# Projections of the second layer as three fp32r products of halves, with jobs moved in the written-out order

## The reference

```python
h = film(rmsnorm(x, norm1_w), cond, film1_w, film1_b)
Q = h @ q_w + q_b
K = h @ k_w + k_b
V = h @ v_w + v_b
scores = jnp.einsum('bnd,bmd->bnm', Q, K) * D ** (-0.5)
attn = jax.nn.softmax(scores, axis=-1)
out = jnp.einsum('bnm,bmd->bnd', attn, V)
x = x_in + (out @ proj_w + proj_b)
```

## Time and profile before

| | us |
|---|---|
| median of 3 runs | 879.87 |
| the profiled execution | 880.76 |
| its span, first to last instruction | 878.9 |
| TensorE busy | 838.7 (95%) |
| VectorE busy | 666.1 (76%) |
| ScalarE busy | 459.4 (52%) |
| POOL busy | 227.3 (26%) |

### The profile page before, as it was taken

One profiled execution on the slowest core, in us unless ns is written; L12 is line 12 of the kernel. 1 busy time (PEld: TensorE's weight loads), 2 busy tenths in 40 slices (PEclk: granted clock), 3 DMA queues, 4 the chain that ended last, 5 costly groups with the idle time before them and its releaser, 6 DMA issues.

```text
span 878.9 us, 13287 instructions
## 1 busy us (share of the span) xinstructions
PE 838.7 (95%) x4978; PEld 521.8 (59%) x4978; DVE 666.1 (76%) x1139; ACT 459.4 (52%) x840; POOL 227.3 (26%) x377
## 2 busy tenths in 40 slices
PE   6999999999999999999989989999999999999994
PEld 3668888958977998887845433333333333333342
DVE  8998657676538577646458879999999999999377
ACT  4646232144332443333232158888878878888760
POOL 4443412202002103112112710233333333333411
PEclk9999999999999999999989969999999999999998
DMA  8613122110000000000597600505050505000002
GB/s 314 252 49 97 55 92 98 49 52 2 1 1 1 1 1 1 2 1 1 168 182 193 252 1 3 92 21 92 21 93 21 92 21 93 23 27 24 27 25 73
DMA packets 29379, 57.40 MB, mean 65 GB/s; under 512 B 7228, under 2 KB 15152, under 8 KB 29314
## 3 DMA queue, kind: packets, MB, share of 16 engines
q1 hardware_dynamic: 22596, 44.40, 19.2%
q0 software_dynamic: 6720, 12.15, 4.7%
HBM read 39.26 MB, written 14.91 MB: 62 GB/s over the span
## 4 chain that ended last, share of the span: by engine, by line
PE 83%; DVE 8%; ACT 5%; POOL 2%; issue 2%; DMA 0%; DVEq 0%; ACTq 0%; POOLq 0%
PE PA L1531 15%; PE PA L1542 15%; PE PD L1327 10%; PE PA L1305 8%; PE PA L1253 7%; PE PD L1502 7%; PE PA L1408 5%; PE PD L1378 4%; PE PA L1246 2%; PE PA L1398 1%; PE PD L1600 1%; DVE NMX L2045 1%; PE PA L1477 1%; ACT R L1107 1%; PE PD L1253 1%
## 5 line engine op out<-in xcount | busy, mean ns | idle before, releaser
L2045 DVE TENSOR_REDUCE NMX<-PD 128x2 f32<-128x1024 f32 x256 | 301.9, 1220 | 25.7 <-PE PD L1502 21.2
L1107 ACT ACTIVATE R<-PA 128x512 f32<-128x512 f32 x512 | 267.0, 603 | 71.6 <-PE PA L1531 69.8
L1531 PE MATMUL PA<-STKR 50*128 50x512 f32 x512 | 185.3, 454 | 3.6 <-ACT R L1107 2.5
L1531 PEld LDWEIGHTS PA<-STKR 50*128 50x128 f32 x512 | 83.2, 188 | 151.7 <-ACT R L1107 139.3
L1502 PE MATMUL PD<-STKR 48*128 48x512 f32 x512 | 150.0, 456 | 4.2 <-DVE NMX L2045 4.1
L1043 ACT ACTIVATE R<-PA,VEC 128x512 f32<-128x512 f32 x64 | 43.8, 687 | 104.1 <-PE PA L1305 91.6
L1327 PE MATMUL PD<-WHR,HSR 128*128 128x256 f32 x512 | 95.3, 285 | 0.5 <-DVE HSR L1918 0.5
L1327 PEld LDWEIGHTS PD<-WHR,HSR 128*128 128x128 f32 x512 | 82.1, 191 | 6.1 <-issue 2.0
L1305 PE MATMUL PA<-XSR,WHR 128*128 128x512 f32 x256 | 81.2, 398 | 3.9 <-issue 2.0
L1502 PEld LDWEIGHTS PD<-STKR 48*128 48x128 f32 x512 | 62.0, 188 | 30.1 <-DVE NMX L2045 13.4
L1327 PE MATMUL PD<-WLR,HSR 128*128 128x256 f32 x256 | 72.4, 283 | 0.0
(11 more groups left out here) (288 smaller groups left out, 1181.3 us busy)
## 6 DMA issues: line engine op xcount, KB each, us to landing
STKR<-qk_terms SPq DMA_DIRECT2D x32, 384.0 KB, 8.8
R<-in_l_w SPq DMA_DIRECT2D x8, 1024.0 KB, 5.0
W<-in_w SPq DMA_DIRECT2D x4, 1024.0 KB, 10.7
qk_terms<-PARTS SPq DMA_DIRECT2D x8, 512.0 KB, 3.4
qk_terms<-PARTS POOLq DMA_DIRECT2D x8, 512.0 KB, 3.8
S<-row_reciprocals POOLq DMA_DIRECT2D x56, 64.0 KB, 2.1
X<-in_x SPq DMA_DIRECT2D x4, 512.0 KB, 8.5
qk_terms<-PARTS SPq DMA_DIRECT2D x8, 256.0 KB, 5.0
```

Source lines behind the costliest of these rows:

```text
L1107: act.activation(PB[:, n % 2, j, :], PA[:, e % NEB, :], ACT.Exp).then_inc(s_exp3, 1)
L1531: pe.matmul(PA[:, e % NEB, :], KS[rows, slot(gg), jj, kt * P:(kt + 1) * P], QS[rows, slot(gg), jj, c * HALF:(c + 1) * HALF], start=True, s ...
L2045: ve.tensor_reduce(out, PD[:, o:o + NROW, :], axis=AX_X, op=ALU.max, negate=True).then_inc(s_mred, 1)
```

## The change

Q, K and V products of layer 1 become three fp32r products of halves. The halves of the tiles go to XSR (the MLPs' tile halves, free at that time), those of the weights to the upper parts of C2 and S2 and back over WA. VectorE gets two new stages, tile_halves and weight_halves, and a subtraction in wv. The stage n1 of batch 0 moves to behind down product 29, wh stands behind 27. The adapter jobs ad and lr are moved later, and three max jobs stand between the Q/K jobs 8 to 15 in place of the end.

```diff
--- before.py
+++ after.py
@@ -103,14 +103,14 @@
 
 assert NLCH == 8 and TWO == P // GCOL
 SCHED = [("nr", 0), ("nn", 0), ("gk", 0), ("ba", 0), ("n0", 0), ("sx", 1), ("bu", 0), ("gg", 0), ("sq", 1), ("cg", 0), ("as", 0), ("bu", 1), ("gr", 0), ("gg", 1),
-         ("an", 0), ("nn", 1), ("ya", 0), ("n0", 1), ("ad", 0), ("gc", 0), ("cg", 1), ("y0", 0), ("yn", 0), ("ad", 1), ("bu", 2),
-         ("ad", 2), ("ws", 0), ("bu", 3), ("yn", 1), ("gk", 1), ("lr", 0), ("bg", 0), ("ma", 0), ("ya", 1), ("lr", 1),
-         ("y0", 1), ("mb", 0)]
-FIRST = mlps(0, "m", {0: [None, ("ws", 1), ("yn", 2), ("yn", 3), None, ("lr", 2)], 4: [("lr", 3)], 6: [("gb", 0)],
+         ("an", 0), ("nn", 1), ("ya", 0), ("n0", 1), ("gc", 0), ("cg", 1), ("y0", 0), ("ad", 0), ("yn", 0), ("bu", 2), ("ad", 1),
+         ("ws", 0), ("bu", 3), ("yn", 1), ("gk", 1), ("bg", 0), ("ma", 0), ("ya", 1), ("ad", 2), ("y0", 1), ("lr", 0), ("mb", 0)]
+FIRST = mlps(0, "m", {0: [None, ("ws", 1), ("yn", 2), ("yn", 3), None, ("lr", 1)], 2: [("lr", 2)], 5: [("lr", 3)], 6: [("gb", 0)],
                       8: [None, None, None, ("lr", 4)], 11: [("lr", 5)], 13: [("lr", 6)], 16: [None, None, None, ("lr", 7)]},
-             {NTILE - 1: [("h0", 0)], B * NTILE - 6: [("wt", 0)], B * NTILE - 4: [("wv", 0)]})
+             {NTILE - 1: [("h0", 0)], B * NTILE - 6: [("wt", 0)], B * NTILE - 5: [("wh", 0)], B * NTILE - 4: [("wv", 0)],
+              B * NTILE - 3: [("n1", 0)]})
 SCHED += FIRST[1:] + [("h0", 1)]
-SCHED += [("n1", 0), ("qk", 0), ("lb", 0), ("att", 0), ("az", 0), ("n1", 1), ("ao", 0), ("qk", 1), ("pr", 0), ("pn", 0),
+SCHED += [("qk", 0), ("lb", 0), ("att", 0), ("az", 0), ("n1", 1), ("ao", 0), ("qk", 1), ("pr", 0), ("pn", 0),
           ("att", 1), ("ws", 2), ("az", 1)]
 SECOND = mlps(1, "n2", {0: [None, ("pr", 1), ("pn", 1)]},
               {NTILE: [("x2", 0)], NTILE + 1: [("a1", 0)], NTILE + 2: [("g", 0)], NTILE + 3: [("a2", 0)], NTILE + 4: [("f2", 0)],
@@ -131,12 +131,16 @@
 
 TURN = {turn_step(m): m for m in range(1, NUNIT)}
 SOLO = turn_step(NUNIT - 1) + 1
-SCHED += weave([("qk3", QJOBS + j) for j in range(QJOBS - 1)], [("mx", EARLY + j) for j in range(QJOBS - 1)])
-EARLY += QJOBS - 1
-assert UNIT == EARLY
-SCHED += [("qk3", 2 * QJOBS - 1), ("mx", EARLY), ("tm", 0)]
-SCHED += weave([("v3", TWO + j) for j in range(TWO)], [("mx", EARLY + 1 + j) for j in range(TWO)])
-SCHED += [("mx", n) for n in range(EARLY + 1 + TWO, LEAD)]
+for j in range(QJOBS):
+    SCHED += [("qk3", QJOBS + j), ("mx", EARLY)]
+    EARLY += 1
+    if j % 2 and j < QJOBS - 1:
+        SCHED.append(("mx", EARLY))
+        EARLY += 1
+    if UNIT < EARLY <= UNIT + 2 and ("tm", 0) not in SCHED:
+        SCHED.append(("tm", 0))
+SCHED += weave([("v3", TWO + j) for j in range(TWO)], [("mx", EARLY + j) for j in range(TWO)])
+SCHED += [("mx", n) for n in range(EARLY + TWO, LEAD)]
 AFTER = {SOLO + 2 * j + i: [(("p3a", "p3")[i], j)] for j in range(TWO - 1) for i in range(2)}
 AFTER[SOLO + TWO - 1] += [("st", 0), ("end", 0), ("ea", 0)]
 AFTER[SOLO + TWO] += [("eb", 0)]
@@ -300,6 +304,9 @@
             R0, XN0, WA0, C20 = 8192, 33024, 37120, 41216
             STKR = at("STKR", R0, [P, NPLACE * 4096])
             PARTS = [at(f"PARTS{u}", o, [P, 2, 2, HALF]) for u, o in enumerate((XN0, WA0))]
+            WAR = at("WAR", WA0, [P, 4, KB, D])
+            C2R = at("C2R", C20, [P, T])
+            S2R = at("S2R", C20 + T, [P, T])
             NMT = at("NMT", C20, [UNIT, NPART, P])
             ONES = at("ONES", C20 + NPART * P, [P, 32])
             VR = at("VR", R0, [P, 2, NT * D])
@@ -401,6 +408,9 @@
                   for n, low in enumerate((QLR, KLR)))
         V = [VR[:, x, :].rearrange("p (t d) -> p t d", t=NT) for x in range(2)]
         PX = R[:, 4096:6144].rearrange("p (s n) -> p s n", s=2)
+        XTR = XSR[:, :].rearrange("p (b k t) -> p b k t", b=B, k=KB)
+        WQKV = [[a.rearrange("p (k n) -> p k n", k=KB), WAR[:, w]]
+                for w, a in enumerate((C2R[:, KB * D:T], S2R[:, KB * D:T], C2R[:, 0:KB * D]))]
         WVT = C2[:, 0:KB * D].rearrange("p (k n) -> p k n", k=KB)
         VBC = S2[:, 0:KB * P].rearrange("p (k m) -> p k m", k=KB)
         X2T = [flat(XN[:, 1]).rearrange("p (k t) -> p k t", k=KB), XT[:, 1]]
@@ -497,6 +507,8 @@
         s_z = sem("states_ready")
         s_zc = sem("states_cos_ready")
         s_zs = sem("states_sin_ready")
+        s_half1 = sem("second_layer_tile_halves_ready")
+        s_whalf = sem("attention_weight_halves_ready")
         s_rowbias = sem("v_bias_in_rows")
         s_qkh = sem("scores_operands_high_ready")
         s_vhi = sem("v_high_ready")
@@ -1361,11 +1373,18 @@
                 m.then_inc(s_afull, 1)
 
             def qk(b):
-                for name, w in (("q", 0), ("k", 1)):
+                pe.wait_ge(s_whalf, 2)
+                terms = [(k, w, x) for k in range(KB) for w, x in TERMS]
+                for name, weights in zip("qk", WQKV):
                     for c in range(NC):
-                        xt_ready(b, "n1", c)
+                        pe.wait_ge(s_half1, (b * NC + c + 1) * KB)
                         for k in range(KB):
-                            project(abank(b, name, c, k), WA[:, w], k * P, b, c, s_afull)
+                            o = abank(b, name, c, k)
+                            for n, (i, w, x) in enumerate(terms):
+                                m = pe.matmul(o, weights[w][:, i, k * P:(k + 1) * P],
+                                              XTR[:, (1 - b, b)[x], i, c * HALF:(c + 1) * HALF],
+                                              start=(n == 0), stop=(n == len(terms) - 1))
+                            m.then_inc(s_afull, 1)
 
             def scores(b, t):
                 if t == 0:
@@ -1383,11 +1402,12 @@
                 if b == 0 and j == 0:
                     evacuated(pe, 0, "wv", 0)
                 o = abank(b, "v1", j)
+                terms = [(k, w, x) for k in range(KB) for w, x in TERMS]
                 for u in range(2):
                     t = 2 * j + u
-                    for k in range(KB):
-                        m = pe.matmul(o[:, u * D:(u + 1) * D], XT[:, b, k, t * P:(t + 1) * P], WA[:, 2, k, :],
-                                      start=(k == 0), stop=(k == KB - 1))
+                    for n, (k, w, x) in enumerate(terms):
+                        m = pe.matmul(o[:, u * D:(u + 1) * D], XTR[:, (1 - b, b)[x], k, t * P:(t + 1) * P], WQKV[2][w][:, k, :],
+                                      start=(n == 0), stop=(n == len(terms) - 1))
                 m.then_inc(s_afull, 1)
 
             def probs_turn(b, t):
@@ -1949,12 +1969,30 @@
                 ve.tensor_copy(VBC.rearrange("p k m -> p (k m)"), bank_of(b, "wt", 1)[:, 0:KB * P]).then_inc(s_aevd, 1)
 
             def wv(b):
-                ve.tensor_copy(WA[:, 2].rearrange("p k d -> p (k d)"), bank_of(b, "wv", 0)).then_inc(s_aevd, 1)
+                high, low = (a.rearrange("p k n -> p (k n)") for a in WQKV[2])
+                o = bank_of(b, "wv", 0)
+                link(ve.tensor_copy(high, o))
+                ve.tensor_tensor(low, o, high.bitcast(F32), ALU.subtract).then_inc(s_aevd, 1)
                 row = BC[:, BP, :]
                 ve.wait_ge(s_bin, 16)
                 ve.tensor_tensor(row, bank_of(b, "wv", 1)[:, 0:D], row, ALU.add).then_inc(s_aevd, 1)
                 evacuated(ve, b, "wv", 1)
                 ve.sem_inc(s_rowbias, 1)
+
+            def weight_halves(_):
+                ve.wait_ge(s_wain, 32)
+                for w in range(2):
+                    high, low = WQKV[w]
+                    link(ve.tensor_copy(high, WA[:, w]))
+                    ve.tensor_tensor(low, WA[:, w], high.bitcast(F32), ALU.subtract).then_inc(s_whalf, 1)
+
+            def tile_halves(b):
+                for _, tag, h, k in turned(b, "n1"):
+                    evacuated(ve, b, tag, h, k)
+                    high, low = (XTR[:, x, k, h * HALF:(h + 1) * HALF] for x in (1 - b, b))
+                    tile = XT[:, b, k, h * HALF:(h + 1) * HALF]
+                    link(ve.tensor_copy(high, tile))
+                    ve.tensor_tensor(low, tile, high.bitcast(F32), ALU.subtract).then_inc(s_half1, 1)
 
             def scores_max(b, t):
                 ve.wait_ge(s_sfull, b * NT + t + 1)
@@ -2120,7 +2158,7 @@
             run({"ws": low_weights, "pn": lambda b: normalise("pr", b, False),
                   "cg": gated_maps, "as": ada_stats, "an": ada_normalise, "ad": hidden_rows, "gc": grouped_columns, "bu": bu,
                  "ya": y0("ya"), "y0": y0("y0"), "ma": split("ma"), "mb": split("mb"), "m": split("m"), "n2": split("n2"), "u0": split("u0"),
-                 "u1": split("u1"), "d0": d0, "h0": h0, "lb": lb, "wt": wt, "wv": wv, "qk": qk, "att": att("att"), "az": att("az"),
+                 "u1": split("u1"), "d0": d0, "h0": h0, "lb": lb, "wt": wt, "wh": weight_halves, "wv": wv, "n1": tile_halves, "qk": qk, "att": att("att"), "az": att("az"),
                  "ao": att("ao"), "pr": pr, "d1": d1,
```

## The result

The changed kernel takes 887.52 us (median of 7 runs, 882.18 to 888.03); the kernel before took 880.42 beside it (7 runs, 879.1 to 882.11). The ratio is 1.0063, 95% interval 1.0044 to 1.0083: 5.5 us slower, and above the forecast range. (The means are 5.6 us apart, the medians 7.1: four of the seven runs of the changed kernel lie at 887.5 to 888.0 and three at 882.2 to 885.3.) The profiled execution took 887.91 us, span 886.1, mean granted clock 0.977 (before 880.76, 878.9 and 0.982).

The account below looks back on a forecast made before the run. Products on TensorE were taken to bound the second layer's stretch (25.5 of 25.7 us busy). Against the profiled 880.76 us, +2.2 +0.9 +1.7 -2.7 -1.9 = +0.2, in the median's terms 880.1 us; range 875.5 to 883.8.

Parts of the forecast that it names:

- Three max jobs: Moved from the end to between Q/K jobs: -3.4 at the end, +1.3 and +0.2 among the jobs, sum -1.9 us.
- It just keeps up: Between the Q/K jobs: VectorE needs 4.8 us for two jobs against TensorE's 4.8; 0.2 put for small waits.
- the clock behind the end: Half clock level at the start of the loop of steps, 9.8 us in the profile, left as it is.
- Batch 0: Second layer: TensorE waits 4.9 us for a bank before K, +0.9 us; clock then at half level, +1.7.
- Batch 1 and behind it: Second layer: Q and K take 11.1 instead of 13.75 us, -2.7 kept; the V saving (0.9 to 1.2) lost.
- Adapter: First layer: +1.2 us ahead of mb's transposes, +1.0 for one more lr product in the MLP, sum +2.2.
- the rival that it does not come: Start of the steps: the half clock level behind the tail does not come; 876.7 us, chance 0.10 including ending soon.
- its other half (it ends soon): Same rival's other case: the half level at the start of the steps ends soon; 876.7 us, shared chance 0.10.
- The forecast's +0.2: Whole kernel: sum of all terms against the profiled 880.76 us; 880.1 us as a median, no measurable change, chance 0.46.
- The rival on the slower side: Batch 0, first Q job's bank: pairs of 1.5 us, wait 6.7 us, second half-clock stretch; 883.6 us, chance 0.22.

Follow-up runs that it names:

- max_only: The kernel before with only the change's three max jobs moved between the Q/K jobs; 883.41 us, ratio 1.0024.
- h0_behind_qk: The changed kernel with h0 of batch 1 moved behind batch 0's Q/K job; 879.81 us, ratio 0.9984.
- products_only: The changed kernel with the adapter jobs and the max jobs back in the order of the kernel before; 881.45 us, ratio 1.0013.
- adapter_early: The kernel before with the adapter jobs in the change's order, except ad 1 ahead of bu 2 again; 887.71 us, ratio 1.0079.
- turn_later: The changed kernel with the turn of the first 16 maxima moved one Q/K job later; 882.03 us, ratio 1.0014.
- adapter_lr_only: The kernel before with only ad 2 and the lr products moved, ad 0 and ad 1 in their old places; 881.45 us, ratio 1.0014.

## Why the prediction was wrong

**Three max jobs: the step that failed.** The prediction had -1.9; the jobs alone measure +2.1. Its reductions were counted rightly: with the turn out of the way they give 1.4 between C and D. "It just keeps up" was worked out for the products and reductions of a pair, as load. The turn of the maxima was not in the working at all. With the three jobs added it stands as the third in a row that takes one of two pairs of banks, and so it waits for the reduction of the first of them and what is queued ahead of that on VectorE: 1.94 us. That this place costs the time is shown: the intervals with the turn here and one Q/K job later don't meet. Behind a wait of that size the clock may fall too: in the kernel after the next four products took 3.65 us instead of 1.9. The 1.3 by which C-D grew is -1.4 for the fewer reductions, 0.9 for the turn's place (max_only and h0_behind_qk against the kernels with the later turn) and 1.8 for the fall. The trace of max_only explains -0.45 without a fall and about +1.3 with one. What remains up to its 2.1 is open. A candidate is a longer half level in the steps (the clock behind the end, below): with the 371.7 us from D to the end that the kernel after and h0_behind_qk have, it would be 2.8 more. No trace of max_only shows it.

**Batch 0: right mechanism, too small.** Predicted +2.6 with the clock; from A to B the kernel after lost 4.77, of which 1.25 is the lr product, so 3.5; products_only alone lost 3.97. Q began 4.6 us behind the transposes, as worked out. What was too small is the wait, 5.11 (4.9 predicted), and above all K, which took 7.8 us in the kernel after and 8.3 in products_only (7.2 by the terms). The cause is confirmed: h0 1 moved by one place, and the wait went to 1.73 and the fall away.

**Batch 1 and behind it: right.** -2.7 predicted; Q and K of batch 1 take 2.83 less, and from B to C kernels with the new products need 216.2 (median of eight), those without 219.6 (of six), so the 2.7 is kept and part of the V saving may be too. The new products cost 0.228 us each in the long row of 48, a little under the 0.231 taken. By the Trainium skill (FP8 and Floating Point Precision, TensorE Precision Notes) a true fp32 product takes four passes; three products of halves against four passes would be 0.75, as an estimate. Here the ratio is 10.92 / 13.75 = 0.79, so the measured rows decide.

**Adapter: right in size and mechanism, with one path missed.** +2.2 predicted, +2.3 alone. Split as predicted (1.2 ahead of mb, 1.0 in the MLP) it measures 1.07 and 1.25. The gelu waits behind bu 2's job on VectorE and W1's halves behind it, as worked out: 55.92 against 55.3, the low half at 58.17 against 57.75 (the terms written there add up to 57.71), VectorE's idle 2.34 against 2.4. What the prediction missed is ad 0's copy: it counted TensorE's 1.49 us wait for ad 0 as removed, and did not follow that copy to who reads it. Behind y0 0's statistics it comes 7 us later, TensorE stands 1.22 us for it, and it makes the plain repair (adapter_early) worse than the fault.

**The clock behind the end: there, but not for nothing.** The prediction left it as it is, a term of 0. The half level came in all 14 traces, so the rival that it does not come is out. Its length differs, though: TensorE worked 13.6 us at it behind D in the kernel after, 10.8 in the kernel before, and 3.4 in max_only and turn_later, so its other half (it ends soon) did happen in kernels with the same shorter end. In the profiled execution D-end is 2.7 of the 7.2 us lost. The shorter end took waiting away from that stretch and left the work in it, which fits; but whether the longer stretch comes from the change or by chance is not shown by one trace each.

**Sum.** In the timed ratios adapter +2.3, products +1.1 and max jobs +2.1 make 5.5, and the change measures 5.5; each of these is known to 1.1 to 1.7 us. The forecast's +0.2 is off mainly by the 4 us of the max jobs and the 1.2 of the products. The rival on the slower side had the right place (the bank of the first Q job) and the wrong price: pairs stayed at 1.06 us (177.49 to 181.75 for four). My list had no case in which two terms were late together.

## What to carry to other kernels

When a product gets cheaper by giving VectorE more to do, list VectorE's queue in order from the new work to the instruction that frees TensorE's bank, and move what nobody waits for behind that instruction: one place was worth 5.6 us here. Then go through the small jobs around each one moved, since they don't show in the load. Count who takes the banks: a third user of two pairs in a row waits for a reduction, though its own data is ready. And follow each copy that comes later to who reads it. Such a wait can cost its length again through the clock. Undo such a change by parts before dropping it; this one, 0.6% slower as a whole, holds a kernel that is 0.7% faster.

## What the hardware showed

- After a wait the clock falls in some executions and not in others. Behind the waits of 4.95 to 5.12 us (four traces: the kernel after, turn_later, products_only, adapter_early) and 8.35 us on TensorE it was at half level each time; behind 1.72 and 1.73 us never, in the three traces that have it; behind 1.93 to 1.95 us it fell in one of three (kernel after: 3.65 us for four products; max_only: 1.96 for the same four).
- How long the half level lasts differs as well. At the start of the steps TensorE worked between 3.4 and 13.7 us at it, in kernels that are alike there (max_only 3.4, h0_behind_qk 13.7), and the stretch from D to the end was 368.2 and 371.7.
- Run times go with the granted clock. The kernel before lay between 877.5 and 884.65 us in 35 runs on one chip, wider than most single effects here; the mean granted clock was 0.987 in its two fastest runs and 0.977 and 0.978 in the two slowest. The stretches between fixed starts tell effects apart where one profile's span does not: adapter_lr_only had a span of 879.1, 0.2 above the kernel before, with 1.25 us of loss in A-B.
